# Moving one subtraction of the first stage from GpSimd to VectorE, which reads it straight from PSUM

## The chip, the cores and the metric

The kernel runs on one core of one Trainium2 chip. The metric is the device time in microseconds (us) of one execution, the median of three runs. The engines are TensorE (PE, with its weight loads as PEld), VectorE (DVE), ScalarE (ACT), GpSimd (POOL) and the DMA queues, which SyncE (SP) and GpSimd issue to.

## The reference, cut to what matters

Four layers are applied to x of shape (8, 128, 64, 64). Only the first one is touched. It is a selective scan over the 4096 positions of each image, with 128 channels and a state of 16:

```python
tn = _ln(t, ln_g, ln_b)
xz = tn @ in_w + in_b
xs, z = (xz[..., :DI], xz[..., DI:])
...
xc = jax.nn.silu(xc)                    # after a causal convolution of 3 taps
dbc = xc @ xproj_w
dt = jax.nn.softplus(dbc[..., :R] @ dt_w + dt_b)
Bm = dbc[..., R:R + N]
Cm = dbc[..., R + N:]
dA = jnp.exp(dt[..., None] * A)
dBx = dt[..., None] * Bm[:, :, None, :] * xc[..., None]
...
h = dA_t * h + dBx_t                    # step by step, y = sum over n of h * C
y = ys.swapaxes(0, 1) + xc * D_ssm
y = y * jax.nn.silu(z)
```

Layers 2 to 4 (line scans, a gated convolution, a deformable convolution) follow and are the same in both kernels.

## The kernel before

`layer0` works through 8 images in 8 chunks of 512 positions (CH), 64 chunks g in all. In a chunk the 16 states n are taken one after another, by five engines that each run their own written-out program:

- TensorE spreads row n of B over 128 partitions into one of four PSUM banks (`spread_B`, three states ahead, L884) and sums the weighted states into `pY` (`sum_state`, L873). In state n of a chunk it sums what `SUM_AT` lists; the last two of a chunk come in states 0 and 1 of the next one.
- ScalarE makes the decay dA of state n + 3 (`decay`, L940).
- VectorE multiplies B by dt * x (`product`, L1007, one state ahead) and scans (L1017). After scan 2 it multiplies the finished `pY` of the chunk before by the gate (`gated`, L999). ScalarE's `direct_term` (L928), in state 3, waits for that product, since it overwrites `pY`.
- GpSimd multiplies state n by C (`weigh`, L979), after scan n, and in state 6 adds the result of the chunk before to the residual (L984).

Beside the states stands the preparation of the next chunk, and of the one after it, in small parts. Tables say in which state an engine does a part: `PE_AT`, `ACT_AT`, `POOL_AT`. VectorE has none. A part is issued in its engine's program order behind the state's own work, so an engine that waits in a part holds back all its states behind it.

The part that matters here: TensorE projects B and C of the next chunk into the PSUM bank `pf[0]`, B twice (partitions 0 to 15 and 32 to 47) and C on partitions 64 to 79. ScalarE, in state 6, in the parts "dt argument" and then "round B, C", does three instructions on dt (L693, L695, L697), copies the bank to `bcs` rounded (L701), and copies it again to `bcf` in full precision (L704), which signals `c_out`. GpSimd, in state 7, subtracts on partitions 32 to 63 the rounded B from the full one ("rest of B, C", L724), so that the matmul that spreads B gets both halves. It signals `blo`. TensorE waits for `blo` ahead of the first `spread_B` of the next chunk, and for `c_out` ahead of the part "centre" (L602), in state 8, which writes `pf[0]` anew. SyncE stores C of `bcf` to memory after `c_out` and loads it back spread over the partitions.

GpSimd's other parts are "softplus" in state 9 (L729, L732), "dt" in 10 (L736), "dt * x" in 11 (L741) and "normalise" in 13 (L720). Counted with the 16 states and the result it issues 23 instructions in a chunk. `after(engine, semaphore, k, lag)` is a wait until the k-th signal less the lag.

Of the kernel before, what the change touches and what calls it, by code (L numbers as in the profile page):

```python
# [16 lines left out]
F32 = mybir.dt.float32  # L17
F32R = mybir.dt.float32r
U32 = mybir.dt.uint32
ALU = mybir.AluOpType  # L20
ACT = mybir.ActivationFunctionType
# [3 lines left out]
B, H, W = 8, 64, 64  # L25
# [4 lines left out]
HALF = 64  # L30
NS = 16
# [8 lines left out]
def after(eng, sem, k, lag=0):  # L40

    eng.wait_ge(sem, k + (1 + CREDIT - lag))
# [456 lines left out]
def layer0(nc, G, x_dram, x1_dram, c_dram):  # L500
# [8 lines left out]
    with ExitStack() as ctx:  # L509
# [26 lines left out]
        rest = sb("m_rest", [P, CH])  # L536
# [3 lines left out]
        dt = sb("m_dtv", [P, 2, CH])  # L540
        dtx = sb("m_dtx", [P, 2, CH])
        sz = sb("m_sz", [P, 4, CH])
        bcf = sb("m_bcf", [P, 2, CH])
        bcs = sb("m_bcs", [P, 2, CH], F32R)
# [7 lines left out]
        pf = [ctx.enter_context(nc.psum_tensor(f"m_pf{i}", [P, CH], F32)) for i in range(2)]  # L552
# [9 lines left out]
        def sem(name):  # L562
# [24 lines left out]
                 10: ["variance"]}  # L587
        ACT_AT = {1: ["norm", "halo"], 3: ["silu"], 6: ["dt argument", "round B, C"], 8: ["log", "pad"], 9: ["centre"],
                  11: ["deviation"]}
        POOL_AT = {7: ["rest of B, C"], 9: ["softplus"], 10: ["dt"], 11: ["dt * x"], 13: ["normalise"]}  # L590
        TWO_AHEAD = ("norm", "halo", "centre", "variance", "deviation", "normalise")
        CONV_AT = {7: 1, 8: 1, 10: 1, 11: 1, 13: 1, 15: 1}
        SUM_AT = {4: (0, 1), 6: (2, 3), 7: (4, 5), 8: (6,), 9: (7,), 10: (8,), 11: (9,), 12: (10,), 13: (11,), 14: (12,),
# [3 lines left out]
        def front_pe(g, b, c, what):  # L597
            pe, par = nc.tensor, c % 2
            if what == "centre":
                after(pe, s.norm, g)  # L600
                after(pe, s.c_out, g, 1)
                pe.matmul(pf[0][:], T.centred[0:HALF, :], xnc[0:HALF, c % 4, :], start=True, stop=True).then_inc(s.p1, 1)  # L602
            if what == "variance":
                after(pe, s.sq, g)
                after(pe, s.xb, g, 1)
                pe.matmul(pf[1][:], G.mean64[0:HALF, :], sq[0:HALF, :], start=True, stop=True).then_inc(s.var, 1)
            if what in ("tap 0", "tap 1", "tap 2"):
                j = int(what[-1])
                if j == 0:
                    after(pe, s.u, g)  # L610
                    after(pe, s.halo, g)
                    after(pe, s.sq, g)
                rows = slice(0, HALF if j == 2 else P)
                mm = pe.matmul(pf[0][:], T.scan_in[rows, j, :], un[rows, par, j:j + CH], start=(j == 0), stop=(j == 2))
                if j == 2:
                    mm.then_inc(s.cv, 1)
            if what == "gate input":
                after(pe, s.lnv, g)
                after(pe, s.u, g)
                pe.matmul(pf[1][:], T.inz[HALF:P, :], un[HALF:P, par, 2:2 + CH], start=True, stop=True).then_inc(s.z, 1)  # L620
            if what == "project B, C":
                after(pe, s.xc, g)
                pe.matmul(pf[0][:], T.bc[:], xc[:, par, :], start=True, stop=True).then_inc(s.bc, 1)
            if what == "project dt":
                after(pe, s.sz, g)
                after(pe, s.xc, g)
                pe.matmul(pf[1][:], T.dt[:], xc[:, par, :], start=True, stop=True).then_inc(s.dtp, 1)

        def front_act(g, b, c, what):
            act, par = nc.scalar, c % 2  # L630
# [67 lines left out]
            if what == "round B, C":  # L698
                after(act, s.bc, g)
                after(act, s.B, 16 * g - 16, 1)  # L700
                act.activation(bcs[:, par, :], pf[0][:], ACT.Copy)  # L701
                act.wait_ge(s.c_stored, 16 * g + (16 + CREDIT - 32))
                after(act, s.blo, g, 2)
                act.activation(bcf[0:HALF + NS, par, :], pf[0][0:HALF + NS, :], ACT.Copy).then_inc(s.c_out, 1)  # L704
            if what == "log":
                after(act, s.e, g)
                after(act, s.dt, g, 1)
# [5 lines left out]
        def front_pool(g, b, c, what):  # L713
            pool, par = nc.gpsimd, c % 2
            if what == "normalise":
                after(pool, s.rstd, g)
                after(pool, s.z, g, 2)
                after(pool, s.cv, g, 2)
                after(pool, s.halo, g, 1)
                pool.tensor_tensor(un[:, par, 2:2 + CH], tc[:], sq[:], ALU.mult).then_inc(s.u, 1)  # L720
            if what == "rest of B, C":
                after(pool, s.c_out, g)
                after(pool, s.HC, NS * (g - 1) + 7)
                pool.tensor_tensor(bcs[32:64, par, :], bcf[32:64, par, :], bcs[32:64, par, :].bitcast(F32),  # L724
                                   ALU.subtract).then_inc(s.blo, 1)
                after(pool, s.blo, g)
            if what == "softplus":
                after(pool, s.r1, g)
                pool.tensor_tensor(rest[:], ea[:], rest[:], ALU.subtract).then_inc(s.r2, 1)  # L729
                after(pool, s.r2, g)  # L730
                after(pool, s.ln, g)
                pool.tensor_tensor(rest[:], rest[:], ln[:], ALU.add).then_inc(s.r3, 1)  # L732
            if what == "dt":
                after(pool, s.r3, g)
                after(pool, s.xb, g)
                pool.tensor_tensor(dt[:, par, :], dt[:, par, :], rest[:], ALU.add).then_inc(s.dt, 1)  # L736
            if what == "dt * x":
                after(pool, s.dt, g)
                after(pool, s.xc, g)
                after(pool, s.U, 16 * g - 16, 1)  # L740
                pool.tensor_tensor(dtx[:, par, :], dt[:, par, :], xc[:, par, :], ALU.mult).then_inc(s.dtx, 1)  # L741

        def program(eng, at, chunk, front, finish, before=lambda: None):

            def parts(n, one_ahead, two_ahead):
                for what in at.get(n, ()):
                    where = two_ahead if what in TWO_AHEAD else one_ahead
                    if where:  # L750
                        front(*where, what)

            def image(b, last):
                def place(c):

                    if c >= NCH:
                        return b * NCH + c, (b + 1) % B, c - NCH
                    return b * NCH + c, b, c
                for c in range(NCH):
                    prev = place(c - 1) if c else (b * NCH - 1, b - 1, NCH - 1) if last else None  # L760
                    chunk(b * NCH + c, b, c, prev, lambda n: parts(n, place(c + 1), place(c + 2)))
            for n in range(NS):
                parts(n, None, (0, 0, 0))
            for n in range(NS):
                parts(n, (0, 0, 0), (1, 0, 1))
            before()
            image(0, False)
            with eng.Fori(1, B) as b:
                image(b, True)
            finish(B * NCH - 1, B - 1, NCH - 1)  # L770

        with nc.Block() as block:
# [199 lines left out]
            def _(pool):  # L972
# [13 lines left out]
                def chunk(g, b, c, prev, parts_ahead):  # L986
                    for n in range(NS):
# [3 lines left out]
                        parts_ahead(n)  # L991
                program(pool, POOL_AT, chunk, front_pool, result)

            @block.vector
            def _(dve):
                def gated(g, c):
                    after(dve, s.sum, NS * g + NS - 1)
                    after(dve, s.sz, g)
                    dve.tensor_tensor(sz[:, c % 4, :], pY[:], sz[:, c % 4, :], ALU.mult).then_inc(s.y, 1)  # L999

                def chunk(g, b, c, prev, parts_ahead):
                    def product(n):
                        m = NS * g + n
                        after(dve, s.B, m)
                        if n == 0:
                            after(dve, s.dtx, g)
                        dve.tensor_tensor(pB[:, n % NB, :], dtx[:, c % 2, :], pB[:, n % NB, :], ALU.mult).then_inc(s.U, 1)  # L1007
                    product(0)
                    for n in range(NS):
                        m = NS * g + n  # L1010
                        if n + 1 < NS:
                            product(n + 1)
                        after(dve, s.U, m)
                        after(dve, s.dA, m)
                        if n % 4 == 0:
                            after(dve, s.HC, m + 3, NS)
                        dve.tensor_tensor_scan(h[:, n, :], dA[:, n % NDA, :], pB[:, n % NB, :],  # L1017
                                               T.zero[:, 0:1] if c == 0 else h[:, n, CH - 1:CH],
                                               ALU.mult, ALU.add).then_inc(s.S, 1)
                        if prev and n == 2:  # L1020
                            gated(*prev[0::2])

                def finish(g, b, c):
                    gated(g, c)
                program(dve, {}, chunk, None, finish)

def layers2_and_3(nc, G, x1_dram, x3_dram, out):
# [830 lines left out]
```

## Time and profile before

| | |
|---|---|
| median of 3 runs | 6879.02 us (6876.97 to 6880.95) |
| profiled execution, first to last instruction (its span, the only time that it has) | 7648.3 us |
| first to last gate product of the first stage, 63 chunk steps | 141.0 to 2121.3 us of that span |
| mean granted TensorE clock, whole span / that stretch | 0.864 / 1.00 of full speed |
| busy in that stretch of 1980.27 us: TensorE, VectorE, ScalarE, GpSimd | 1889.58, 1841.95, 1600.15, 1801.05 us |

The profile is of one execution, which took longer than the timed ones. Starts are in us from its first instruction. An instruction's duration runs to its end, and the next one on the same engine can start a little before that; the step from start to start is what a full engine pays. In brackets behind a row stands the idle time ahead of it and what ended it.

### The profile page before, as it was taken

The numbers are of one execution on the slowest core, as the hardware profiler recorded it, in microseconds if no ns is written. First come the engines' busy times: TensorE is split into PE (matmuls) and PEld (weight loads), VectorE is DVE, ScalarE is ACT, GpSimd is POOL, SyncE is SP. The second block draws the span as 40 slices with busy tenths as digits, with TensorE's granted clock in tenths as the row PEclk, the third lists the DMA queues.
The fourth block names the chain that finished last, engine by engine and source line by source line (L and its number), as shares of the span: only waits on it lengthen the run. The fifth ranks groups of instructions, "written<-read, shape, count | busy, mean of one in ns | idle before, by whom it ended". The sixth has DMA issues, their size and how long they took to land. (4 is left out here: it accounts for less than half of the span.)

```text
span 7648.3 us, 89071 instructions
## 1 busy us (share of the span) xinstructions
PE 5717.8 (75%) x21147; PEld 3269.1 (43%) x21147; DVE 5490.3 (72%) x12779; ACT 3409.0 (45%) x7221; POOL 4111.0 (54%) x3871
## 2 busy tenths in 40 slices
PE   5999999999989999999865565655656565565442
PEld 2444444444478888888532222322223232232111
DVE  6999999999967777778565666556566665665556
ACT  4888888888855211111233333333333333333333
POOL 4999999999910001000055555655556565565663
PEclk9999999999999999999987676877778777687665
DMA  5445444444420000000156555555555665555567
GB/s 193 170 179 180 167 169 172 170 168 167 168 87 3 3 0 23 0 0 0 42 164 198 164 184 178 168 183 168 180 180 172 193 184 183 178 176 179 178 182 265
DMA packets 306397, 1093.60 MB, mean 143 GB/s; under 512 B 56560, under 2 KB 58639, under 8 KB 264604
## 3 DMA queue, kind: packets, MB, share of 16 engines
q0 software_dynamic: 187440, 625.23, 27.1%
q1 hardware_dynamic: 118516, 464.08, 17.0%
q14 instruction: 359, 2.94, 0.1%
q8 instruction: 82, 1.34, 0.1%
HBM read 997.72 MB, written 91.37 MB: 142 GB/s over the span
## 5 line engine op out<-in xcount | busy, mean ns | idle before, releaser
L1281 POOL DMA_INDIRECT d_ring<-corner_table,d_idx_now x2304 | 2212.2, 960 | 1635.9 <-issue 950.2
L1481 PE MATMUL d_ps_s<-small,d_mix 128*128 128x128 f32 x2304 | 489.6, 350 | 1544.2 <-DVE d_mix L1653 1010.5
L979 POOL TENSOR_TENSOR X<-X 128x512 f32<-128x512 f32 x1024 | 1289.7, 1277 | 168.3 <-DVE X L1017 150.9
L1481 PEld LDWEIGHTS d_ps_s<-small,d_mix 128*128 128x128 f32 x2304 | 327.8, 176 | 2071.0 <-issue 1089.5
L1653 DVE SCALAR_TENSOR_TENSOR d_acc<-d_ring,d_w_now,d_mix 128x128 f32<-128x128 f32 x2304 | 660.9, 354 | 694.3 <-ACT d_mix L1327 321.5
L1017 DVE TENSOR_TENSOR_SCAN X<-X,m_pB 128x512 f32<-128x512 f32 x896 | 1132.4, 1269 | 0.0
L873 PE MATMUL m_pY<-X,small 128*128 128x512 f32 x2048 | 1040.4, 605 | 90.3 <-POOL X L979 90.2
L277 PE MATMUL prop_ps<-prop_parts,prop_w_hi 128*128 128x480 f32 (+4 forms) x4536 | 1099.8, 387 | 4.6 <-DVE prop_parts L286 4.6
L1327 ACT ACTIVATE d_mix<-d_ring,d_w_now 128x128 f32<-128x128 f32 x2304 | 732.3, 390 | 719.1 <-DMA d_ring<-corner_table,d_idx_now 659.1
L277 PEld LDWEIGHTS prop_ps<-prop_parts,prop_w_hi 128*128 128x128 f32 x4536 | 816.0, 188 | 133.4 <-DVE prop_parts L286 5.4
L1411 PE MATMUL d_ps_out<-d_samp,d_dcn_w 128*128 128x512 f32 x1152 | 832.0, 815 | 7.9 <-ACT X L1314 5.8
L1007 DVE TENSOR_TENSOR m_pB<-m_dtx,m_pB 128x512 f32<-128x512 f32 x1024 | 693.0, 678 | 92.2 <-PE m_pB L884 69.3
L884 PE MATMUL m_pB<-m_bcs,m_pick 128*128 128x512 f32 x1027 | 758.9, 739 | 0.1
L940 ACT ACTIVATE X<-m_dtv,m_A 128x512 f32<-128x512 f32 x1027 | 688.5, 713 | 96.3 <-POOL m_dtv L736 74.7
L225 ACT ACTIVATE prop_sum<-prop_ps 128x256 f32<-128x256 f32 x504 | 194.5, 386 | 1169.4 <-PE prop_ps L277 1169.4
L1653 DVE SCALAR_TENSOR_TENSOR d_mix<-d_ring,d_w_now,d_acc 128x128 f32<-128x128 f32 x2304 | 646.8, 340 | 85.1 <-remote 45.7
L1653 DVE SCALAR_TENSOR_TENSOR d_acc<-d_ring,d_w_now,d_acc 128x128 f32<-128x128 f32 x2304 | 649.5, 348 | 43.5 <-DVE d_acc L1653 26.4
L272 PEld LDWEIGHTS prop_ps<-prop_parts,prop_w_lo 128*128 128x128 f32 x4536 | 598.3, 189 | 51.8 <-issue 9.8
L272 PE MATMUL prop_ps<-prop_parts,prop_w_lo 128*128 128x240 f32 (+4 forms) x4536 | 604.1, 277 | 16.4 <-POOL prop_w_lo L200 9.6
L873 PEld LDWEIGHTS m_pY<-X,small 128*128 128x128 f32 x2048 | 363.7, 188 | 469.8 <-POOL X L979 281.6
L1440 PE MATMUL l_ps_a<-l_xn,l_w 128*128 128x512 f32 x896 | 462.9, 648 | 24.1 <-DVE l_gate L1541 24.1
L200 POOL TENSOR_TENSOR prop_w_lo<-prop_raw,prop_w_hi 128x1152 fp32r<-128x1152 f32 x4 | 10.6, 2648 | 793.1 <-ACT prop_w_hi L218 793.1
(231 smaller groups left out, 7744.8 us busy)
## 6 DMA issues: line engine op xcount, KB each, us to landing
X<-c_scratch SPq DMA_DIRECT2D x256, 1024.0 KB, 4.9
d_ring<-corner_table,d_idx_now POOLq DMA_INDIRECT x2304
corner_table<-d_tT SPq DMA_DIRECT2D x120, 256.0 KB
X<-in_x SPq DMA_DIRECT2D x8, 2048.0 KB, 15.2
m_res<-in_x SPq DMA_DIRECT2D x64, 256.0 KB, 4.6
x_scratch<-m_res SPq DMA_DIRECT2D x64, 256.0 KB, 2.1
x_scratch<-X SPq DMA_DIRECT2D x8, 2048.0 KB
b_x<-x_scratch POOLq DMA_DIRECT2D x16, 1024.0 KB, 11.7
```

What stands on the lines that cost most here:

```text
L272: pe.matmul(ps[s][:, 1, a:b, :], w_lo[:, d % 2, k * P:(k + 1) * P], parts[s][:, 0, a + k - MID:b + k - MID, :], start=(k == MID), stop=Fal ...
L277: mm = pe.matmul(ps[s][:, :, a:b, :], w_hi[:, d % 2, k * P:(k + 1) * P], parts[s][:, :, a + k - MID:b + k - MID, :], start=False, stop=(k ...
L873: pe.matmul(pY[:], G.ident, hc[:, n % NHC, :], start=False, stop=(n == NS - 1), skip_group_check=True).then_inc(s.sum, 1)
L884: pe.matmul(pB[:, n % NB, :], T.pick[:, n:n + 1].to_broadcast([P, P]), bcs[:, par, :], start=True, stop=True).then_inc(s.B, 1)
L979: pool.tensor_tensor(hc[:, n % NHC, :], h[:, n, :], Cb[:, n, :], ALU.mult).then_inc(s.HC, 1)
L1007: dve.tensor_tensor(pB[:, n % NB, :], dtx[:, c % 2, :], pB[:, n % NB, :], ALU.mult).then_inc(s.U, 1)
L1017: dve.tensor_tensor_scan(h[:, n, :], dA[:, n % NDA, :], pB[:, n % NB, :], T.zero[:, 0:1] if c == 0 else h[:, n, CH - 1:CH], ALU.mult, ALU. ...
L1281: pool.indirect_dma_start(out=ring[:, m % RING, :], out_offset=None, in_=flat, in_offset=bass.IndirectOffsetOnAxis(ap=idx_now[:, c % 2, m: ...
L1327: r0 = act.activation(R[:, k % 3, t, :], ring[:, m % RING, 0:P], ACT.Copy, scale=w_now[:, c % 2, 4 * m:4 * m + 1])
L1411: pe.matmul(ps_out[:], dcn_w[:, k, :], samp[:, k % 3, :], start=(k == 0), stop=(k == TAPS - 1)).then_inc(s_dcn, 1)
L1481: turned = pe.transpose(ps_s[k % 3][:, t, :], R[:, k % 3, t, :], G.ident)
L1653: mixed = dve.scalar_tensor_tensor(R[:, k % 3, t, :] if corner == 3 else acc[:, t, :], ring[:, m % RING, corner * P:(corner + 1) * P], w_n ...
```

## The change

GpSimd's part "rest of B, C" goes, with its two waits for GpSimd's own work around it. VectorE gets a table `DVE_AT` with one part, "rest of B", in state 7: after product 8 and scan 7 it waits for `c_out`, reads B in full precision from the PSUM bank `pf[0]`, subtracts the rounded one and signals `blo`. ScalarE's second copy now takes only the 16 partitions of C and no longer waits for an older `blo`. TensorE's "centre" waits for `blo` instead of `c_out`.

```diff
-        POOL_AT = {7: ["rest of B, C"], 9: ["softplus"], 10: ["dt"], 11: ["dt * x"], 13: ["normalise"]}
+        POOL_AT = {9: ["softplus"], 10: ["dt"], 11: ["dt * x"], 13: ["normalise"]}
+        DVE_AT = {7: ["rest of B"]}
...
             if what == "centre":
                 after(pe, s.norm, g)
-                after(pe, s.c_out, g, 1)
+                after(pe, s.blo, g, 1)
...
                 act.wait_ge(s.c_stored, 16 * g + (16 + CREDIT - 32))
-                after(act, s.blo, g, 2)
-                act.activation(bcf[0:HALF + NS, par, :], pf[0][0:HALF + NS, :], ACT.Copy).then_inc(s.c_out, 1)
+                act.activation(bcf[HALF:HALF + NS, par, :], pf[0][HALF:HALF + NS, :], ACT.Copy).then_inc(s.c_out, 1)
...
-            if what == "rest of B, C":
-                after(pool, s.c_out, g)
-                after(pool, s.HC, NS * (g - 1) + 7)
-                pool.tensor_tensor(bcs[32:64, par, :], bcf[32:64, par, :], bcs[32:64, par, :].bitcast(F32),
-                                   ALU.subtract).then_inc(s.blo, 1)
-                after(pool, s.blo, g)
...
+        def front_dve(g, b, c, what):
+            dve, par = nc.vector, c % 2
+            if what == "rest of B":
+                after(dve, s.c_out, g)
+                dve.tensor_tensor(bcs[32:64, par, :], pf[0][32:64, :], bcs[32:64, par, :].bitcast(F32),
+                                  ALU.subtract).then_inc(s.blo, 1)
...
                         if prev and n == 2:
                             gated(*prev[0::2])
+                        parts_ahead(n)
...
-                program(dve, {}, chunk, None, finish)
+                program(dve, DVE_AT, chunk, front_dve, finish)
```

## Rows read from the trace of the kernel before

**Rows 1.** Busy time in one stretch, first to last gate product of the stage.
```profile
core 0: us, PE busy (x) PEld busy (x) DVE busy (x) ACT busy (x) POOL busy (x), PEclk, DMA share, GB/s
141.04:2121.31 1980.27, 1889.58 (x4910) 807.24 (x4908) 1841.95 (x2073) 1600.15 (x2633) 1801.05 (x1448) 1.00 0.48 170
```

**Rows 2.** Timeline of VectorE: start, duration, instruction, idle before.
```profile
989.69 0.69 DVE L999 TENSOR_TENSOR m_sz<-m_pY,m_sz 128x512 f32<-128x512 f32 x1 [1.44 <-PE m_pY L873]
...
1021.14 0.69 DVE L999 TENSOR_TENSOR m_sz<-m_pY,m_sz 128x512 f32<-128x512 f32 x1 [1.44 <-PE m_pY L873]
1021.75 0.69 DVE L1007 TENSOR_TENSOR m_pB<-m_dtx,m_pB 128x512 f32<-128x512 f32 x1
1022.34 1.27 DVE L1017 TENSOR_TENSOR_SCAN X<-X,m_pB 128x512 f32<-128x512 f32 x1
...
1029.42 1.27 DVE L1017 TENSOR_TENSOR_SCAN X<-X,m_pB 128x512 f32<-128x512 f32 x1
1030.61 0.67 DVE L1007 TENSOR_TENSOR m_pB<-m_dtx,m_pB 128x512 f32<-128x512 f32 x1
1031.19 1.27 DVE L1017 TENSOR_TENSOR_SCAN X<-X,m_pB 128x512 f32<-128x512 f32 x1
```

**Rows 3.** Timeline of GpSimd, parts of two chunks.
```profile
1000.09 1.28 POOL L979 TENSOR_TENSOR X<-X 128x512 f32<-128x512 f32 x1
1001.52 1.28 POOL L724 TENSOR_TENSOR m_bcs<-m_bcf,m_bcs 32x512 fp32r<-32x512 f32 x1
1003.04 2.52 POOL L979 TENSOR_TENSOR X<-X 128x512 f32<-128x512 f32 x2 [0.24 <-PE m_pY L873]
1005.51 1.28 POOL L729 TENSOR_TENSOR m_rest<-m_ea,m_rest 128x512 f32<-128x512 f32 x1
...
1011.78 1.26 POOL L741 TENSOR_TENSOR m_dtx<-m_dtv,m_xc 128x512 f32<-128x512 f32 x1
...
1016.71 6.18 POOL L979 TENSOR_TENSOR X<-X 128x512 f32<-128x512 f32 x5
1023.77 1.27 POOL L979 TENSOR_TENSOR X<-X 128x512 f32<-128x512 f32 x1 [0.88 <-DVE X L1017]
...
1029.08 1.27 POOL L979 TENSOR_TENSOR X<-X 128x512 f32<-128x512 f32 x1 [0.50 <-DVE X L1017]
1030.31 1.28 POOL L984 TENSOR_TENSOR m_res<-m_res,m_fin 128x512 f32<-128x512 f32 x1
```

**Rows 4.** Timeline of TensorE: centre, then the end of the chunk.
```profile
1002.76 0.69 PE L602 MATMUL m_pf<-m_xnc,m_centred 64*128 64x512 f32 x1
...
1018.03 1.13 PE L873 MATMUL m_pY<-X,small 128*128 128x512 f32 x2 [0.25 <-POOL X L979]
1018.99 1.02 PE L614 MATMUL m_pf<-m_un,m_scan_in 128*128 128x512 f32 x2
1019.45 0.79 PE L884 MATMUL m_pB<-m_bcs,m_pick 128*128 128x512 f32 x1
1020.08 1.02 PE L873 MATMUL m_pY<-X,small 128*128 128x512 f32 x2
```

**Rows 5.** Timeline of ScalarE, from the gate product to the copy that signals `c_out`.
```profile
1021.87 0.69 ACT L928 ACTIVATE m_pY<-m_xc,m_D 128x512 f32<-128x512 f32 x1 [3.65 <-DVE m_sz L999]
1022.58 1.28 ACT L685 ACT_TABLE_LOAD   x1
...
1031.02 0.59 ACT L704 ACTIVATE m_bcf<-m_pf 80x512 f32<-80x512 f32 x1
```

**Rows 6.** The same two instructions where an image starts.
```profile
1084.77 0.69 ACT L928 ACTIVATE m_pY<-m_xc,m_D 128x512 f32<-128x512 f32 x1 [3.65 <-DVE m_sz L999]
...
1094.22 0.59 ACT L704 ACTIVATE m_bcf<-m_pf 80x512 f32<-80x512 f32 x1
```

**Rows 7.** VectorE's small steps ahead of the stage, each waiting for its forerunner.
```profile
62.06 0.16 DVE L106 TENSOR_TENSOR gn_varL<-gn_mvL 128x8 f32<-128x8 f32 x1
62.26 0.17 DVE L108 TENSOR_TENSOR gn_momentsL<-gn_mvL,gn_varL 128x8 f32<-128x8 f32 x1
```

## The prediction

> **What bounds the kernel now.** I read the busy times of the stage first. No engine is full: TensorE is busy for 95%, VectorE for 93%, GpSimd for 91% of the stretch, at a granted clock of 1.00, the upper of TensorE's two levels, 2.4 GHz [rows 1]. So a loop over several engines sets the pace, and the timelines must show it. From the gate product of one chunk to that of the next are 31.45 us [rows 2]; over the stage the mean is 1980.27 / 63 = 31.43 us [rows 1], so the chunk that I take stands for nearly all.
>
> I count from the start of a gate product (t = 0, at 1021.14) and use the chunk before it (t = 0 at 989.69) where its rows are the ones shown.
>
> - VectorE goes without a stop from the gate product to scan 6. Scan 3 starts at 1.20, and each further pair of product and scan takes 1.77, as from scan 7 at 1029.42 to scan 8 at 1031.19 [rows 2]. Scan 6 thus starts at 1.20 + 3 x 1.77 = 6.5.
> - GpSimd waits for scans 3, 4, 5 and 6. Its state 6 starts at 7.94, which is 1.42 behind the start of the scan, and this is its last wait for VectorE in the chunk [rows 3].
> - From there GpSimd is full: 1.235 from start to start (five states in 6.18 us). It reaches state 9 at 1003.04 + 1.235 = 1004.27, t = 14.58. State 14 starts 12.44 later, at 1016.71, and ends at 17.96 on that clock [rows 3].
> - TensorE starts to sum state 14 at 1018.03, then does a convolution tap and a spread of B, then sums state 15 from 1020.08 to 1021.10. The gate product follows at 1021.14 [rows 2, 4]. That is 3.11 us from the sum of state 14 on.
>
> This loop closes: 14.58 + 12.44 + 1.25 + 0.07 + 3.11 = 31.45. VectorE has slack in it: it stood idle for 1.44 before the gate product [rows 2].
>
> **What the change removes.** The step on GpSimd from its state 7 (1000.09) to its state 8 (1003.04) is 2.95 us, where without the part it would be 1.235. The part with its two drains costs 1.72 us, all on the loop above [rows 3]. Were nothing added, state 9 would start at 7.94 + 4 x 1.235 = 12.9; but it needs scan 9, which starts at 8.28 + 2 x 1.77 = 11.82, so at 11.82 + 1.42 = 13.24. That alone would be 1.34 us a chunk, 84 us in 63.
>
> **What it adds.** VectorE's part stands behind scan 7, which starts at 8.28 and ends at 9.55 [rows 2]. It then waits for `c_out`. ScalarE's second copy starts at 1031.02 and ends at 1031.61, t = 10.47 [rows 5]. ScalarE gets there no earlier, for its work is chained to the same gate product: the direct term waited for it (3.65 us idle), starts at 0.73, and from there to the copy ScalarE has no idle time. The shorter copy (16 partitions for 80) saves nothing that I count: its length is 512 columns as before. The wait that it loses, for a `blo` of two chunks ago, was long met.
>
> So VectorE, which never waited in this place, waits for 10.51 - 9.47 = 1.04 us (0.04 from an end to the start of its waiter, as between TensorE and the gate product; 9.47 is when product 9 started until now). Behind the wait stand product 9, scan 8, product 10, scan 9; and GpSimd's states 8 and 9 wait for these scans.
>
> Then the subtraction itself. The trace has no VectorE instruction that starts on partition 32. The nearest row is the gate product, one input in PSUM, the other and the output in SBUF, 0.69 us [rows 2]. Its lower bound is its start-to-start step of 0.61, with scan 8 another 0.58 or 0.59 behind product 9: scan 8 at 10.51 + 0.61 + 0.58 = 11.70. The upper bound takes away both overlaps: 0.69 for the subtraction and 0.69 for product 9, each with 0.03 behind it, as between two steps of which one waits for the other [rows 7]: scan 8 at 10.51 + 0.72 + 0.72 = 11.95. All overlaps in the rows are between instructions that start on the same partition, so I take the upper value, for this instruction and its neighbours do not.
>
> The Trainium skill bears on the choice (VectorE: DVE Perf Modes, "Two Vector instructions with no wait between them"): an instruction whose operands start in another group of 32 partitions than those of its forerunner is held until all earlier VectorE work has finished. By that rule the subtraction holds product 9 and its output holds scan 8, and the sum would be the upper one; without it, the lower. No row of before shows either.
>
> **The sum.** Scan 9 starts 1.77 behind scan 8, at 13.72, and GpSimd's state 9 at 13.72 + 1.42 = 15.14. GpSimd itself is there earlier (state 8 at 13.37 behind scan 8, state 9 at 14.6 at best). From state 9 on all is as before, so a chunk takes 15.14 - 14.58 = 0.56 us more, 32.01 for 31.45. With the lower bound state 9 starts at 14.89: 0.31 more. Of the 1.72 that GpSimd is spared, 1.34 could have been used, as worked out above; scan 8 moves from 10.05 to 11.95, by 1.90: 1.04 of wait and 0.86 of subtraction and lost overlap. 1.90 - 1.34 is the 0.56.
>
> Other waits, costed at nothing: VectorE's product 0 needs "dt * x", whose start is 7.51 behind state 9 and end 8.77, so 23.91; VectorE comes to it at 13.72 + 5 x 1.77 + 2 x 1.19 = 24.95. It reaches the gate product at about 30.9, 1.1 before it can start at 32.0. TensorE's "centre" now waits for `blo`, at 11.2; it starts at 13.07 today [rows 4], so 1.9 us cover it. SyncE's C store follows `c_out`, which does not move against the gate product.
>
> At the start of an image `c_out` comes at 1094.81 - 1084.04 = 10.77, 0.30 later [rows 6], if the direct term at 1084.77 stands 0.73 behind its gate product as in the other chunk. These 8 steps pay 0.56 + 0.30, about 0.9. So 55 x 0.56 + 8 x 0.9 = 31 + 7 = 38 us, and with the lower bound 55 x 0.31 + 8 x 0.6 = 22 us. Against the profiled execution this is 7648.3 to 7686. The profiled execution is 769 us longer than the median of the runs, 6879.0, and I can't see where. The stage's mean chunk is within 0.02 us of the one taken and its clock is full, so I take the 38 us over as they are, less 2 for that doubt: 6915.
>
> **Rivals.**
>
> *The overlaps stay* (lower bound above): 6879 + 22 = 6901. For it: every pair of neighbours in [rows 2] overlaps by 0.08. Against it: none of them changes the starting partition.
>
> *The wait is hidden, and the change gains.* This is the case if `c_out` is there when scan 7 ends, at 9.55 or earlier; it would have to come 0.9 us sooner. Then scan 8 starts at 9.55 + 1.44 = 10.99, state 9 at 14.18, and a chunk saves 0.40 (with overlaps 0.72): 63 x 0.40 = 25, so 6854, down to 6833. Against it is that ScalarE's chain from the direct term to the copy is full and starts at the gate product, wherever that moves. This is the point from which it decides: 9.9 for `c_out` breaks even.
>
> *No change.* GpSimd, with 1.72 us less to do, absorbs the wait: state 9 stays at 14.58. It needs the subtraction to cost VectorE under 0.3 us, half the nearest row, or a step of GpSimd behind state 9 to shrink. 6879, within 14 us.
>
> *A second wait joins.* If another engine falls behind through VectorE's delay (TensorE's spread of B waits for scans four back, and B banks number four), a chunk could pay 1.0 or more: 6879 + 63 = 6942. TensorE is idle only 1.4 us in 31.4 [rows 1], but the spreads that follow scan 8 have two states to spare.
>
> **How the numbers follow.** A measurement of this kernel tells about 0.2%, 14 us, from no change. Forecast (6905 to 6928) 0.45; overlaps stay 0.24; no change 0.13; gain 0.10; second wait 0.08. Slower is 0.45 + 0.24 + 0.08 = 0.77, same 0.13, faster 0.10. The range leaves out the gain, the second wait and the lower part of no change: 6882 to 6930.
>
> **What the profile would show.** Right: VectorE idle for 1.0 before the subtraction, released by ScalarE's copy; the gate product every 32.0 us (lower bound: 31.76); GpSimd waiting for scans 8 and 9 where it waited for none; scan 8 starting 1.44 (1.19) behind the subtraction. Wrong: no idle time before the subtraction (then it gains), a chunk under 31.45, or a new long wait on TensorE or at product 0. What would make it wrong is above all a `c_out` that comes sooner against the gate product than now.

## The result and the profile after

| | before | after |
|---|---|---|
| median of 5 runs | 6879.02 us (6876.97 to 6880.95) | 6926.11 us (6925.29 to 6929.95) |
| profiled execution, span | 7648.3 us | 6923.5 us |
| first to last gate product of the first stage | 1980.27 us | 2027.14 us |
| one ordinary chunk of it | 31.45 us | 32.07 us |

The ratio is 1.007, with a 95% interval of 1.0059 to 1.0081: the change makes the kernel slower by 47 us. In the profiles the first stage is longer by 2027.14 - 1980.27 = 46.9 us, which is all of it. The two spans must not be compared as wholes. Behind the first stage, whose granted clock is 1.00 in both, the profiled execution of before took 5527 us at a granted clock of 0.81 and that of after 4754 us at 0.87, with the same instructions. So the 769 us for which the prediction had no place lie behind the first stage. On one of the chips used below the unchanged kernel takes 7619 us (median), so the profiled execution of before is like the ones there; why they are longer was not tried.

The stage as a whole, first to last gate product of the kernel after (columns as in [rows 1]):

```profile
142.06:2169.20 2027.14, 1916.86 (x4910) 809.04 (x4908) 1878.12 (x2135) 1620.82 (x2633) 1723.32 (x1385) 1.00 0.47 166
```

GpSimd's work fell by 78 us and VectorE's rose by 36, against [rows 1], and still the stage is longer: every engine has more idle time. The timeline of VectorE after, in one chunk, answers to [rows 2]:

```profile
1042.72 0.69 DVE L1000 TENSOR_TENSOR m_sz<-m_pY,m_sz 128x512 f32<-128x512 f32 x1 [1.01 <-PE m_pY L874]
...
1051.00 1.27 DVE L1018 TENSOR_TENSOR_SCAN X<-X,m_pB 128x512 f32<-128x512 f32 x1
1053.33 0.68 DVE L741 TENSOR_TENSOR m_bcs<-m_pf,m_bcs 32x512 fp32r<-32x512 f32 x1 [1.07 <-ACT m_bcf L704]
1054.05 0.70 DVE L1008 TENSOR_TENSOR m_pB<-m_dtx,m_pB 128x512 f32<-128x512 f32 x1
1054.78 1.28 DVE L1018 TENSOR_TENSOR_SCAN X<-X,m_pB 128x512 f32<-128x512 f32 x1
...
1056.56 1.27 DVE L1018 TENSOR_TENSOR_SCAN X<-X,m_pB 128x512 f32<-128x512 f32 x1
...
1074.79 0.69 DVE L1000 TENSOR_TENSOR m_sz<-m_pY,m_sz 128x512 f32<-128x512 f32 x1 [1.04 <-PE m_pY L874]
```

The gate product starts at 1042.72; counted from it, scan 7 ends at 9.55. VectorE stands idle for 1.07 us until ScalarE's second copy ends, and starts the subtraction at 10.61. Product 9 follows 0.72 behind it and scan 8 another 0.73 behind that: no overlap at either, where [rows 2] has 0.08. Scan 8 starts at 12.06, where it started at 10.05 [rows 2]. The next gate product stands at 32.07, again with 1.04 of idle time before it, for 1.44. The line of the subtraction tells that VectorE waits there in each chunk: 102.4 us in all, 64 times. Of that, 33.05 us are one wait ahead of the stage's first gate product; in the stage the wait is 1.06 to 1.07, and 1.36 at each image's start.

```profile
L741 DVE TENSOR_TENSOR m_bcs<-m_pf,m_bcs x65: 682/683/685, 97.4 to 2148.5; 32x512 fp32r<-32x512 f32 x65
its engine sat idle before it (us, times) until:
  ACT m_bcf L704: 102.4, 64
```

GpSimd's timeline answers to [rows 3]:

```profile
1053.12 1.27 POOL L980 TENSOR_TENSOR X<-X 128x512 f32<-128x512 f32 x1
1056.14 1.28 POOL L980 TENSOR_TENSOR X<-X 128x512 f32<-128x512 f32 x1 [1.75 <-DVE X L1018]
1057.90 1.28 POOL L980 TENSOR_TENSOR X<-X 128x512 f32<-128x512 f32 x1 [0.49 <-DVE X L1018]
1059.13 1.29 POOL L723 TENSOR_TENSOR m_rest<-m_ea,m_rest 128x512 f32<-128x512 f32 x1
```

The part is gone between its states 7 and 8, and in its place stands a wait of 1.75 us for scan 8. State 9 starts at 15.18, where it started at 14.58. Behind it nothing differs: 15.18 + 16.89 = 32.07, and 14.58 + 16.87 = 31.45.

ScalarE's two copies answer to [rows 5]:

```profile
1052.11 0.59 ACT L702 ACTIVATE m_bcs<-m_pf 128x512 fp32r<-128x512 f32 x1
1052.71 0.59 ACT L704 ACTIVATE m_bcf<-m_pf 16x512 f32<-16x512 f32 x1
1053.33 1.34 ACT L941 ACTIVATE X<-m_dtv,m_A 128x512 f32<-128x512 f32 x2
```

The second copy starts 0.60 behind the first, where the step before was 0.48, and ends at 10.58 for 10.47. Its successor stands 0.62 behind it, for 0.47. The second copy now starts on partition 64. The kernel before shows the same loss at an image's start:

```profile
1097.21 0.71 ACT L711 ACTIVATE m_rest<-m_rest,m_minus 128x512 f32<-128x512 f32 x1
1097.94 0.26 ACT L659 ACTIVATE m_xn<-m_zero 64x66 f32<-64x66 f32 x1
1098.21 1.70 ACT L656 ACTIVATE m_xn<-m_xb,m_shift_hw,m_scale_hw 64x512 f32<-64x512 f32 x2
1099.94 0.72 ACT L940 ACTIVATE X<-m_dtv,m_A 128x512 f32<-128x512 f32 x1
```

L659 writes from partition 64 on, the two of L656 from 0 and from 64, L940 from 0 again. Each starts just behind its forerunner's end, where most neighbours on ScalarE start 0.1 us ahead of it. The number of partitions is not it: the copy on 80 partitions behind the one on 128, both from 0, kept its overlap in before.

### The profile page after: what moved, and what is told of

Same layout as the page of the kernel before. It is cut to its first block and busy times, and to the rows that moved or that the text cites. A ratio compares the mean times of both kernels' runs of the same rounds, so it can differ in the third digit from the quotient of the medians.

```text
span 6923.5 us, 88988 instructions
## 1 busy us (share of the span) xinstructions
PE 5606.3 (81%) x21147; PEld 3196.7 (46%) x21147; DVE 5520.1 (80%) x12844; ACT 3450.1 (50%) x7221; POOL 4024.5 (58%) x3806
## 5 line engine op out<-in xcount | busy, mean ns | idle before, releaser
L1483 PE MATMUL d_ps_s<-small,d_mix 128*128 128x128 f32 x2304 | 458.5, 332 | 976.5 <-DVE d_mix L1655 975.7
L1483 PEld LDWEIGHTS d_ps_s<-small,d_mix 128*128 128x128 f32 x2304 | 298.8, 166 | 1510.6 <-DVE d_mix L1655 870.8
L1413 PE MATMUL d_ps_out<-d_samp,d_dcn_w 128*128 128x512 f32 x1152 | 783.0, 770 | 0.0
L885 PE MATMUL m_pB<-m_bcs,m_pick 128*128 128x512 f32 x1027 | 740.6, 722 | 2.3 <-DVE X L1018 2.0
```

The lines of the kernel that those rows point to most:

```text
L885: pe.matmul(pB[:, n % NB, :], T.pick[:, n:n + 1].to_broadcast([P, P]), bcs[:, par, :], start=True, stop=True).then_inc(s.B, 1)
L1413: pe.matmul(ps_out[:], dcn_w[:, k, :], samp[:, k % 3, :], start=(k == 0), stop=(k == TAPS - 1)).then_inc(s_dcn, 1)
L1483: turned = pe.transpose(ps_s[k % 3][:, t, :], R[:, k % 3, t, :], G.ident)
```

## The experiments

Each ratio is to runs of before on the same chip. The second set of four (e5 to e8) ran on a chip on which the kernel before takes 7.6 ms. The first stage's ordinary chunks there are as elsewhere (e8 repeats those of after), so the stage's length and its chunks, from the profiles, are what compares across sets. The ordinary chunk is one step from gate product to gate product, read in the middle of the stage; the median of the 49 is within 0.01 us of it. Under "image starts" stand the six chunk steps over an image's start behind the first loop turn: 31.5 us before (the first of them 32.3).

| run | ratio to before, 95% interval | stage, us | ordinary chunk | image starts |
|---|---|---|---|---|
| before | | 1980.3 | 31.45 | 31.5 |
| after | 1.007 (1.0059 to 1.0081) | 2027.1 | 32.07 | 33.0 to 33.4 |
| e1 ScalarE's parts swapped | 0.9991 (0.9982 to 1.0) | 1972.3 | 31.04 | 33.7 to 34.2 |
| e2 partitions 0 to 31 | 1.004 (1.0027 to 1.0054) | 2013.0 | 31.79 | 33.0 to 34.9 |
| e3 in state 8 | 0.9984 (0.9975 to 0.9993) | 1970.8 | 31.05 | 33.4 to 33.9 |
| e4 no subtraction | 0.9903 (0.9887 to 0.9918) | 1916.2 | 30.07 | 33.7 to 33.8 |
| e5 signal at the first copy | 1.0005 (0.9982 to 1.0029) | 1989.4 | 31.48 | 32.4 to 32.7 |
| e6 GpSimd, partitions 0 to 31 | 0.9988 (0.9961 to 1.0016) | 1970.4 | 31.00 | 34.0 to 34.3 |
| e7 state 9, centre 9, partitions 0 to 31 | 0.9916 (0.9886 to 0.9946) | 1921.1 | 30.30 | 32.4 to 32.8 |
| e8 after, loop written out | 1.0055 (1.0031 to 1.0079) | 2021.5 | 32.07 | 32.35 |
| e9 e7, loop written out | 0.9908 (0.9893 to 0.9923) | 1910.3 | 30.31 | 30.64 |
| e10 e6, C load later | 0.9962 (0.9948 to 0.9976) | 1953.7 | 30.97 | 31.4 to 31.6 |
| e11 e7, C load later | 0.9901 (0.9886 to 0.9916) | 1914.8 | 30.31 | 31.5 to 31.7 |
| e12 after, C load later | 1.0065 (1.0051 to 1.0079) | 2022.3 | 32.07 | 32.45 |

My theory was that of the prediction: the place of the wait in the loop and the lost overlaps set the price. The rivals were that VectorE is simply too full, so that one more instruction costs what it takes wherever it stands, and that GpSimd's part had been hidden.

**e1, `c_out` sooner.**

```diff
-                  6: ["dt argument", "round B, C"]
+                  6: ["round B, C", "dt argument"]
```

> The changed kernel, but ScalarE does 'round B, C' ahead of 'dt argument' in state 6, so c_out comes about 1.66 us sooner against the gate product (8.9 for 10.58), before scan 7 ends at 9.55. If the loop runs through VectorE's wait for c_out: no idle time before the subtraction, which starts at 9.58; scan 8 at 11.0, GpSimd's state 9 at 14.1 for 15.18, a chunk 31.0 us for 32.07, 6926 - 66 = 6860. If VectorE is simply too full with one more instruction and the wait costs nothing of its own, the subtraction starts sooner but the chunk stays at 32.07: 6926. If the later dt argument makes the decays or softplus late: a wait on ScalarE's work in GpSimd's state 9 and a chunk above 31.0.

The second copy ends at 8.91. VectorE's timeline in e1, counted from a gate product at 1016.49:

```profile
1024.77 1.27 DVE L1018 TENSOR_TENSOR_SCAN X<-X,m_pB 128x512 f32<-128x512 f32 x1
1026.07 0.68 DVE L741 TENSOR_TENSOR m_bcs<-m_pf,m_bcs 32x512 fp32r<-32x512 f32 x1
1026.79 0.70 DVE L1008 TENSOR_TENSOR m_pB<-m_dtx,m_pB 128x512 f32<-128x512 f32 x1
1027.52 1.28 DVE L1018 TENSOR_TENSOR_SCAN X<-X,m_pB 128x512 f32<-128x512 f32 x1
```

No wait is left, and VectorE does the same instructions. The chunk is 31.04, as worked out, 1.03 less than after. So VectorE's total work is not the bound. The row also shows the subtraction 0.03 behind scan 7's end and not 0.08 before it: its own start is held too. The time, though, is 6877.64 and not 6860, since the image starts are 2.2 to 2.7 us worse than in before.

**e2, another group of partitions.** B lies in both groups of rows, so the subtraction can be made on either.

```diff
-                dve.tensor_tensor(bcs[32:64, par, :], pf[0][32:64, :], bcs[32:64, par, :].bitcast(F32),
+                dve.tensor_tensor(bcs[0:32, par, :], pf[0][0:32, :], bcs[0:32, par, :].bitcast(F32),
```

> The changed kernel, but the subtraction is made on partitions 0 to 31 in place of 32 to 63 (B lies on both, rounded, and the spread adds the two, so rounded and rest change places and the sum is the same). Everything else and the amount of work are the same. If a VectorE instruction that starts on another partition group than its neighbours loses the overlap with them: product 9 now starts 0.61 behind the subtraction (0.72 before) and scan 8 0.59 behind it (0.73), a chunk 31.8 for 32.07, 6926 - 16 = 6910. If the lost overlap comes from the wait for c_out or from the PSUM read: no difference, 6926. The wait of 1.06 stays in either case.

VectorE's timeline in e2:

```profile
1045.33 0.68 DVE L741 TENSOR_TENSOR m_bcs<-m_pf,m_bcs 32x512 fp32r<-32x512 f32 x1 [1.06 <-ACT m_bcf L704]
1045.94 0.67 DVE L1008 TENSOR_TENSOR m_pB<-m_dtx,m_pB 128x512 f32<-128x512 f32 x1
1046.53 1.26 DVE L1018 TENSOR_TENSOR_SCAN X<-X,m_pB 128x512 f32<-128x512 f32 x1
```

The steps are 0.61 and 0.59 for 0.72 and 0.73, the chunk 31.79 for 32.07. The wait and the PSUM read are the same in both, so it is the starting partition that took the overlaps. These were the two ends of the prediction's bound.

**e3, the part one state later.**

```diff
-        DVE_AT = {7: ["rest of B"]}
+        DVE_AT = {8: ["rest of B"]}
```

> The changed kernel, with VectorE's part in state 8 in place of 7: scan 8 then starts at 10.05 as in the kernel before, and the subtraction at 11.36, when c_out (10.58) is there. If it is the wait at this place that costs: no idle time before the subtraction, scan 9 at 12.8, GpSimd's state 9 at 14.1, a chunk 31.0, 6861. If VectorE's work as such is the bound: 6926. If blo, now at 12.1, holds TensorE's centre: idle time on TensorE at about 13 and something in between.

31.05, with no idle time before the subtraction, which started at 11.35, and none on TensorE at its centre. As in e1 the image starts took away what the chunks gave: 0.9984.

**e4, no subtraction at all.** The rest of B is not formed, so B is summed from two rounded copies.

```diff
-                after(dve, s.c_out, g)
-                dve.tensor_tensor(bcs[32:64, par, :], pf[0][32:64, :], ...
-                                  ALU.subtract).then_inc(s.blo, 1)
...
-                        after(pe, s.blo, g)
+                        after(pe, s.c_out, g)
```

> The changed kernel without the subtraction on any engine, so B's rest isn't formed; TensorE waits for c_out where it waited for blo. It shows what taking the part from GpSimd is worth by itself. By the prediction's working GpSimd's state 9 then starts at 13.2, behind scan 9, and a chunk takes 30.1, 84 us less than before: 6795. TensorE has 30.0 us of work in a chunk, so it may take over as the bound and leave some 30.2 to 30.4: 6800 to 6815. If GpSimd's part was hidden all along: about 6879.

A chunk takes 30.07, 1.38 less than before, where the prediction had 1.34. GpSimd's state 9 starts at 13.17, behind scan 9 (13.24 worked out). So GpSimd's part had been on the loop. Of its 1.72 us, 1.38 come off the chunk; scan 9 holds back the rest.

**e5, the wait cut to the first copy.**

```diff
-                act.activation(bcs[:, par, :], pf[0][:], ACT.Copy)
+                act.activation(bcs[:, par, :], pf[0][:], ACT.Copy).then_inc(s.rounded, 1)
...
-                after(dve, s.c_out, g)
+                after(dve, s.rounded, g)
...
                 after(pe, s.blo, g, 1)
+                after(pe, s.c_out, g, 1)
```

> The changed kernel, but ScalarE signals after its first copy (the rounded one), and VectorE waits for that instead of c_out; TensorE's centre waits for both. The first copy ends at 9.98 in the changed kernel, the second at 10.58. If the place in the loop is the wait: the subtraction starts at 10.0, idle 0.45 before it for 1.06, scan 8 at 11.47, a chunk 31.48 for 32.07, so about 36 us less than the changed kernel and no difference from the kernel before. If the wait were covered elsewhere: no difference from the changed kernel.

```profile
1035.59 0.68 DVE L743 TENSOR_TENSOR m_bcs<-m_pf,m_bcs 32x512 fp32r<-32x512 f32 x1 [0.47 <-ACT m_bcs L704]
```

The wait is 0.47, the subtraction starts at 10.02, 0.59 sooner than after the change, and the chunk is 31.48, 0.59 shorter.

**e6, GpSimd's part without its drains, on partitions 0 to 31.** The kernel before, with

```diff
-                after(pool, s.HC, NS * (g - 1) + 7)
-                pool.tensor_tensor(bcs[32:64, par, :], bcf[32:64, par, :], bcs[32:64, par, :].bitcast(F32),
+                pool.tensor_tensor(bcs[0:32, par, :], bcf[0:32, par, :], bcs[0:32, par, :].bitcast(F32),
                                    ALU.subtract).then_inc(s.blo, 1)
-                after(pool, s.blo, g)
```

> The kernel before, with GpSimd keeping its part, but on partitions 0 to 31 in place of 32 to 63 (rounded and rest change places, the sum is the same) and without the two waits for its own work around it. It prices the drains alone. If the drains are on the loop as the prediction has it: from GpSimd's state 7 to 8 it takes 2.47 us for 2.95, a chunk 30.97 for 31.45, 63 x 0.48 = 30 us less than before. If the drains were only the row's rounding or hidden: no difference. The image starts may take about 2 us more each, as in the first four runs, which would leave about 18 us.

GpSimd's timeline in e6:

```profile
1024.57 1.27 POOL L977 TENSOR_TENSOR X<-X 128x512 f32<-128x512 f32 x1
1025.81 1.26 POOL L723 TENSOR_TENSOR m_bcs<-m_bcf,m_bcs 32x512 fp32r<-32x512 f32 x1
1027.04 2.51 POOL L977 TENSOR_TENSOR X<-X 128x512 f32<-128x512 f32 x2
```

From state 7 to state 8 it takes 2.47 for 2.95 us, and the chunk is 31.00. That is 0.45 to 0.48 us a chunk. The run takes the drains out and moves the partitions at once, so it doesn't price the drains alone. That it is the drains is an inference from the rows: in [rows 3] the part starts 0.15 behind its forerunner's end and its follower 0.24 behind its own, each at a wait; here each starts 0.03 ahead of it. By its time, though, e6 can't be told from before: the image starts took 34.0 to 34.3 us.

**e7, the part behind the last scan that GpSimd's state 9 waits for.** Partitions 0 to 31 as in e2, and

```diff
-        PE_AT = {... 8: ["centre"],
+        PE_AT = {... 9: ["centre"],
...
-        DVE_AT = {7: ["rest of B"]}
+        DVE_AT = {9: ["rest of B"]}
```

> The changed kernel with VectorE's part in state 9, behind scan 9, TensorE's centre in state 9 too, and the subtraction on partitions 0 to 31. Nothing that GpSimd's state 9 waits for is then behind the part. GpSimd's state 9 starts at 13.2, as without any subtraction, and a chunk takes 30.1, like that run, if TensorE's later centre costs nothing; 30.4 if the variance matmul now waits for ScalarE. With the image starts as in the first four runs this is 50 to 65 us less than before. If VectorE's total work counts as such, 0.6 us a chunk more than without the subtraction: 30.7.

30.30, between the 30.1 and the 30.7. GpSimd's state 9 starts at 13.17, as in e4, so the 0.23 over e4 arises behind it. VectorE has no idle time before the gate product any more; its only wait in the chunk is 0.49 us for a spread of B, so TensorE is late there. Why, the rows of TensorE tell. In e4, as in before and after, centre in state 8 ran beside two matmuls of the gated convolution (L892), each of the two pairs starting within 0.01 us:

```profile
1003.83 0.69 PE L892 MATMUL m_pO<-m_xn,m_low 64*128 64x512 f32 x1
1003.83 0.69 PE L603 MATMUL m_pf<-m_xnc,m_centred 64*128 64x512 f32 x1
1004.36 0.59 PE L892 MATMUL m_pO<-m_xn,m_low 64*128 64x512 f32 x1
1004.37 0.59 PE L603 MATMUL m_pf<-m_xnc,m_centred 64*128 64x512 f32 x1
```

In e7, in state 9, it stands alone:

```profile
1006.80 1.12 PE L894 MATMUL m_pO<-m_xn,m_low 64*128 64x512 f32 x2
...
1009.14 1.12 PE L603 MATMUL m_pf<-m_xnc,m_centred 64*128 64x512 f32 x2
1010.20 0.50 PE L885 MATMUL m_pB<-m_bcs,m_pick 128*128 128x512 f32 x1
```

Over the stage all 126 matmuls of centre start beside one of L892's in e4, and none beside one of L894's in e7. So moving centre costs TensorE 1.06 us (1009.14 to 1010.20) in each chunk, and in e4 TensorE was idle for only 0.37 us of one. The 0.23 is then no price of the subtraction on VectorE, which the expectation had put at up to 0.6. No run moves centre alone, so this stays read from rows and not tested.

**e8, VectorE's loop over the images written out.** The first seven runs left one thing open, the image starts. They stood 1 us over the forecast after the change, and 2 to 3 us over before in e1, e4 and e6, whose VectorE has nothing in common that before lacks: in e6 it runs the program of before.

```diff
-            with eng.Fori(1, B) as b:
-                image(b, True)
+            if eng is nc.vector:
+                for b in range(1, B):
+                    image(b, True)
+            else:
+                with eng.Fori(1, B) as b:
+                    image(b, True)
```

> The changed kernel with VectorE's loop over the images written out (no branch at an image's start; the other engines keep theirs). The chunk steps over an image's start took 33.3 us in the changed kernel where 32.4 was worked out, and VectorE stood idle for 2 to 3 us behind its last scan there. If that is VectorE's turn of its loop: the steps fall to 32.5, as at the first image's end, which has no branch, 6 us less in all. If another engine's turn holds it: no change.

The steps are 32.35 or 32.36, all six, and the ordinary chunks stay. What was over the forecast of 32.3 is VectorE's branch.

**e9, the same in e7.**

> The run with VectorE's part in state 9, centre in state 9 and partitions 0 to 31, with VectorE's loop over the images written out. Chunks stay at 30.3; the six steps over an image's start fall from 32.4 to 32.8 to about 30.8, as at the first image's end: 11 us less than that run, the first stage 1910 us for 1980 before, so 70 us less than the kernel before on the same chip. If the branch isn't what costs there: 59 us less.

30.64 for 32.4 to 32.8, and a stage of 1910.3 us, the shortest of all.

**e10, the load of C out of the way.** Why does the same branch cost 1.1 us in before and 3.9 in e6? These are the rows of VectorE around it in before and then in e6, with the idle time behind the last scan of the image:

```profile
1106.01 2.44 DVE L1017 TENSOR_TENSOR_SCAN X<-X,m_pB 128x512 f32<-128x512 f32 x2
1109.65 0.70 DVE L1007 TENSOR_TENSOR m_pB<-m_dtx,m_pB 128x512 f32<-128x512 f32 x1 [1.20 <-issue]
```

```profile
1104.44 0.70 DVE L1005 TENSOR_TENSOR m_pB<-m_dtx,m_pB 128x512 f32<-128x512 f32 x1 [3.85 <-PE m_pB L882]
```

The DMA queues tell more. Q14 carries instructions, q1 SyncE's loads (packets, MB, share of 16 engines). In before, the first half microsecond of the load of C, 1107.0 to 1107.5, and then the next two:

```profile
q1 hardware_dynamic: 15, 0.12, 129.5%
q14 instruction: 1, 0.01, 5.8%
...
q1 hardware_dynamic: 88, 0.72, 88.3%
```

```profile
q1 hardware_dynamic: 124, 1.02, 95.8%
...
q1 hardware_dynamic: 20, 0.03, 8.6%
q14 instruction: 4, 0.03, 8.6%
```

```diff
-                        after(sp, s.HC, NS * g + 4 * q + 3, NS)
+                        after(sp, s.HC, NS * g + (13 if q == 2 else 4 * q + 3), NS)
```

> The run with GpSimd's part on partitions 0 to 31 without drains, with the third of the four loads of C issued after GpSimd's state 13 in place of 11. In that run VectorE stood idle for 3.6 to 3.9 us at each image's start, the kernel before for 1.1, with the same program on VectorE; the load of C began 0.5 us earlier against it, and the instruction queue's packets landed only when that load was through. If code loading stands behind the load of C: the load now begins at 25, behind the packets, VectorE's idle time falls to about 1 us or less, the steps from 34.2 to 31.3, 17 us in all. If the length of the turn has nothing to do with the load: 3.6 to 3.9 again.

In e10, with the image's gate product at 1069.71, the row of VectorE and then the queues from 1092.21 to 1094.21:

```profile
1095.22 1.29 DVE L1005 TENSOR_TENSOR m_pB<-m_dtx,m_pB 128x512 f32<-128x512 f32 x2 [1.10 <-PE m_pB L882]
```

```profile
q14 instruction: 2, 0.02, 3.0%
```

Two packets, with no load beside them, and VectorE goes on after 1.10 us for 3.85. The image starts fell from between 34.0 and 34.3 us to between 31.4 and 31.6, and e6's gain is now measured: 0.9962. The row names TensorE's spread as the releaser in both; it had been done before.

The time of the load is not all that counts. In e4 and e7 it begins at the same 21.7 us behind the gate product and the packet behind it starts at 24.4 to 24.7, yet VectorE is idle for 2.9 to 3.1 us in e4 and for 1.6 to 2.1 in e7. Why stays open.

**e11, the same in e7.**

> The run with VectorE's part in state 9, centre in state 9 and partitions 0 to 31, with the third load of C issued after GpSimd's state 13. Chunks stay at 30.3. If code loading stands behind the load of C, the steps over an image's start fall from 32.4 to 32.8 to about 31, 10 us less than that run and as good as the written-out loop; if not, they stay.

The steps fell to 31.5 to 31.7, not quite to 31, and the kernel takes 6812.67 us for 6880.41. The stage in e11 (columns as above):

```profile
141.79:2056.56 1914.77, 1913.77 (x4910) 849.03 (x4908) 1868.40 (x2135) 1608.54 (x2633) 1721.76 (x1385) 1.00 0.50 176
```

TensorE is busy for 1913.77 of 1914.77 us, at a granted clock of 1.00. It has become the bound of the stage in this order of work. It is no floor for the kernel: in e4 the same 4910 matmuls, with centre in its old place beside L892, were busy for 1882.71 us.

**e12, the same in the changed kernel.**

> The changed kernel with the third load of C issued after GpSimd's state 13. Chunks stay at 32.07. The steps over an image's start took 33.0 to 33.4; with VectorE's loop written out they took 32.35. If code loading stands behind the load of C, VectorE's idle time behind its last scan falls from 2.0 to about 1 and the steps to 32.4, 6 us less than the changed kernel. If not: 33.3 again.

32.45 for 33.0 to 33.4, VectorE's idle time there 0.8 to 1.0 for 1.6 to 2.1, and a stage of 2022.3. The ratio, 1.0065, is not distinguishable from that of after; the steps are.

## Why the prediction was right, point by point

**The loop now.** Right. e4 shows GpSimd's part to be worth 1.38 us a chunk (forecast 1.34), and e6 that 0.45 to 0.48 of it go with the drains and the partitions.

**The wait for `c_out`.** Right in place and nearly in size: 1.07 for 1.04. e1 takes it away, e5 cuts it to 0.47, e3 goes around it, and each moves the chunk as its working says.

**The cost of the subtraction.** The upper bound was the right one: 0.72 and 0.73 for 0.72 and 0.72. e2 shows the lower one, 0.61 and 0.59, by the starting partition alone. The subtraction's own start is held too: without a wait it stands 0.03 us behind its forerunner's end in e1 and e3, and 0.09 ahead of it in e7, where it lies on partitions 0 to 31. The Trainium skill (VectorE: DVE Perf Modes, "Two Vector instructions with no wait between them") states that an instruction whose operands start in another group of 32 partitions than the last ones read or written in the same memory is held until every earlier VectorE instruction has finished. The runs agree: the instruction, its successor and the next one that writes to SBUF start 0.03 to 0.04 us behind their forerunner's end.

**"`c_out`, which does not move against the gate product".** Wrong by 0.11 us. The second copy came 0.12 later behind the first. It now starts on partition 64, and the rows of before show that loss at an image's start, where ScalarE's starting partition changes too, but no run takes it alone. I had counted its length and not its step. On the other side GpSimd followed scan 9 by 1.34, not 1.42. Together the chunk came to 32.07 for 32.01.

**The sum.** Forecast 38 us (36 after a rebate for doubt), measured 46.9 in the profile and 47.1 in the medians. The measured 6926.1 lies near the upper end of the range, 6930: the loop and the wait were right, the sum 9 us short. The rebate had no ground: the doubt behind it was over time spent behind the first stage. The 49 ordinary chunks of the looped images gave 30.0 us (1570.9 - 1540.9; forecast 27.4). The six of the first image gave 5.0 (forecast 3.4): before, they took 31.22, after, 32.06 as all others. Why they were shorter before was not tried. The eight image starts gave 11.9 (263.9 - 252.0), where 7 were forecast, and this is the term that was most off. "These 8 steps pay 0.56 + 0.30" left out VectorE's loop branch. Before, the branch's 1.1 us fell into the slack of 1.0 before the gate product (that is what the first image's end shows, which has no branch; it is not 1.44, since VectorE waits 1.02 for a spread of B there); after, it was 1.63 to 2.07 and the slack 1.02, as e8 shows without the branch. Each step of after is e8's 32.36 plus what its branch has over 1.02: 1.63 gives 32.97 (measured 32.99), 2.07 gives 33.41 (33.42). e8 and e12 both give steps of 32.35 to 32.45, which is what the working had.

**The rivals.** The gain needed `c_out` 0.9 us sooner; e1 brought it 1.67 sooner, and the chunk became shorter than before, by 0.41 (0.40 worked out). No second wait joined: TensorE's centre started at 13.07, as before, and product 0 didn't wait in an ordinary chunk.

## What to carry to other kernels

Freeing an engine is worth nothing if the work then waits in the middle of the loop on the engine that took it. Time the arrival of its input against the instruction it stands behind, and put it behind the last instruction that somebody waits for; here two states made the difference between 47 us lost and, with the partitions changed, centre moved along and the load of C moved, 68 us gained. When something is moved along, look at what it ran beside: centre lost its partner, and TensorE became full. Keep the starting partition of neighbouring instructions the same. And when ordinary iterations improve as worked out and the total does not, look at the loop's turn.

## What was not expected of the hardware

- ScalarE's rows show no overlap of two instructions where the starting partition changes, as on VectorE: a step of 0.60 for 0.48 us between two copies of 512 columns.
- VectorE stood idle for 0.8 to 3.9 us at its loop's branch, by what was on the DMA engines then. In e6 no instruction packet started for 3.1 us while a load of C ran (1.02 MB in 3 us, 95.8% of the engines), and then four did within 0.3 us. A saving of 0.45 us on GpSimd went with a branch on VectorE 2.5 to 2.8 us longer; moving the load took that back (e10).
- Two fp32 matmuls of 64 rows each, one on the lower half of the partitions and one on the upper, started together (1003.83 both) and cost TensorE 1.06 us less a chunk than apart (e4 against e7).
- GpSimd's subtraction on 32 partitions took 1.26 us, as one on 128 does.
